# Output stores and x loads issued per half row of 128 tokens instead of per whole row

## The reference

```python
q = heads(x @ W_q)
probs_t = softmax(q @ heads(text @ W_k).T * scale)            # 73 text tokens
text_out = probs_t @ heads(text @ W_v)
attn_scores = q @ heads(ip @ W_k_ip).T * scale                # 4 ip tokens
sem = l2norm(probs_t @ text) @ l2norm(ip).T
probs_ip = softmax(attn_scores + 0.5 * sem) * spatial_mask
out = (text_out + probs_ip @ heads(ip @ W_v_ip)) @ W_out + b_out
out = out + x                                                 # the residual
```

## Time and profile before

| | before |
|---|---|
| time, median of 3 runs | 1032.5 us (1031.4 to 1037.69) |
| profiled execution, time | 1031.25 us |
| profiled execution, span | 1029.5 us |
| granted clock of the matrix engine, mean | 0.988 of full speed |
| matrix engine busy | 975.6 us (95%) |
| DVE, ACT, POOL busy | 795.9, 705.6, 640.5 us |
| queue q1 (all DMAs that SP issues) | 178.62 MB, 84.2% of 16 engines |
| output stores, x loads in the main loop | 64 and 56, 320 KB each |

### The profile page before, as it was taken

One profiled execution on the slowest core, in us unless ns is written; L12 is line 12 of the kernel. 1 busy time (PEld: TensorE's weight loads), 2 busy tenths in 40 slices (PEclk: granted clock), 3 DMA queues, 4 the chain that ended last, 5 costly groups with the idle time before them and its releaser, 6 DMA issues.

```text
span 1029.5 us, 24562 instructions
## 1 busy us (share of the span) xinstructions
PE 975.6 (95%) x7604; PEld 795.8 (77%) x7604; DVE 795.9 (77%) x2401; ACT 705.6 (69%) x2315; POOL 640.5 (62%) x1899
## 2 busy tenths in 40 slices
PE   7986788999999999999999999999999999999877
PEld 5755566888878888888878888888878888888755
DVE  4375678888878787888878888878888888887861
ACT  1355678777677777768767777777777777787720
POOL 1112467777676667667666767766766677676750
PEclk9999989999999999999999999999999999999989
DMA  9845989879799998888899999888989979778852
GB/s 301 316 139 138 193 152 169 172 167 186 159 190 177 188 190 174 164 176 172 158 189 194 189 167 184 160 177 168 178 179 202 180 169 186 138 160 147 159 109 89
DMA packets 483871, 180.26 MB, mean 175 GB/s; under 512 B 449517, under 2 KB 461855, under 8 KB 483740
## 3 DMA queue, kind: packets, MB, share of 16 engines
q1 hardware_dynamic: 483708, 178.62, 84.2%
q10 hardware_dynamic: 32, 0.07, 0.0%
HBM read 42.34 MB, written 27.22 MB: 68 GB/s over the span
## 4 chain that ended last, share of the span: by engine, by line
PE 77%; DMA 4%; DVE 3%; SPq 3%; ACT 2%; issue 2%; POOL 1%; POOLq 0%; DVEq 0%; ACTq 0%
PE ps_O L1164 26%; PE ps_Q L1198 25%; PE ps_S L1122 12%; PE ps_U L1184 11%; DMA pts<-ph 3%; PE ps_M L1138 3%; ACT pr L905 1%; SPq L825 1%; SPq L795 1%; DMA x_in<-in_x_dram 1%; SPq L785 0%; DVE pr L1060 0%; DVE n L1072 0%; POOL ph L987 0%; DVE w_sem L1055 0%
## 5 line engine op out<-in xcount | busy, mean ns | idle before, releaser
L987 POOL TENSOR_TENSOR ph<-pr,ph 128x220 f16<-128x220 f32 (+1 forms) x640 | 273.8, 459 | 136.5 <-ACT ph L917 136.2
L905 ACT ACTIVATE pr<-ps_S,bias 128x73 f32<-128x73 f32 x1280 | 290.1, 339 | 89.0 <-DVE bias L1021 87.0
L1164 PE MATMUL ps_O<-wo_hi,aT 128*128 128x320 f16 x1280 | 295.1, 302 | 5.6 <-DVE x_in L1006 3.5
L1198 PE MATMUL ps_Q<-xT,wq_hi 128*128 128x512 f32 x800 | 280.6, 416 | 5.9 <-DVE qT L994 5.7
L917 ACT ACTIVATE ph<-pr 128x292 f16<-128x292 f32 x640 | 234.2, 440 | 5.5 <-DMA pts<-ph 0.4
L1164 PE MATMUL ps_O<-wo_lo,aT 128*128 128x320 f16 x640 | 192.7, 301 | 0.0
L1184 PE MATMUL ps_U<-xm,pts 128*128 128x110 f16 (+1 forms) x2560 | 159.5, 213 | 17.9 <-DMA pts<-ph 15.4
L1198 PEld LDWEIGHTS ps_Q<-xT,wq_hi 128*128 128x128 f32 x800 | 146.5, 191 | 33.6 <-DVE qT L994 7.0
L1184 PEld LDWEIGHTS ps_U<-xm,pts 128*128 128x128 f16 (+1 forms) x2560 | 145.1, 98 | 34.9 <-issue 12.4
L1164 PEld LDWEIGHTS ps_O<-wo_hi,aT 128*128 128x128 f16 x1280 | 125.7, 98 | 57.4 <-DVE x_in L1006 4.0
L1122 PEld LDWEIGHTS ps_S<-kbd,qT 128*128 128x128 f32 x960 | 149.9, 189 | 23.2 <-issue 9.2
(11 more groups left out here) (185 smaller groups left out, 1235.3 us busy)
## 6 DMA issues: line engine op xcount, KB each, us to landing
out_dram<-x_in SPq DMA_DIRECT2D x64, 320.0 KB, 2.6
x_in<-in_x_dram SPq DMA_DIRECT2D x56, 320.0 KB, 3.2
pts<-ph SPq DMA_TRANSPOSE x320, 3.3
aT<-in_L_xattn_W_k_dram SPq DMA_DIRECT2D x5, 512.0 KB, 8.7
w_ip<-in_L_xattn_W_k_ip_dram SPq DMA_DIRECT2D x1, 2560.0 KB, 11.6
w_v<-in_L_xattn_W_v_dram SPq DMA_DIRECT2D x1, 2560.0 KB, 18.9
w_ip<-in_L_xattn_W_v_ip_dram SPq DMA_DIRECT2D x1, 2560.0 KB, 9.3
x_in<-in_x_dram SPq DMA_DIRECT2D x2, 1280.0 KB, 12.2
```

Source lines behind the costliest of these rows:

```text
L905: last = nc.scalar.activation(pr[p % P_RING][:, j, h, :], sc[:, j, h, 0:T], ACT.Exp, bias=bias[p % 2][:, j, h:h + 1], scale=SCALE)
L987: nc.gpsimd.tensor_tensor(lo, full[:, :, t0:t1], one[:, :, 0, t0:t1], ALU.subtract).then_inc(pl_ready, 1)
L1164: last = nc.tensor.matmul(o_bank[half % 2][:, 0:HALF], stationary, moving, start=(k, a, b_) == O_MMS[0], stop=(k, a, b_) == O_MMS[-1])
L1198: last = nc.tensor.matmul(ps_Q[:], wq[a][:, c, k * P:(k + 1) * P], xT[(CC * i + c) % XT_RING][b_][:], start=(c, a, b_) == Q_MMS[0], stop=( ...
```

## The change

Stores and loads are issued by halves: 128 partitions with 1280 bytes each, 160 KB, eight of each per tile. `STORE_AT` now has a step for each of the eight halves, one step behind the step in which DVE adds it, and `LOAD_AT` a step for each half of x, one step behind the store that frees its place. The last store and the last load of a tile stay in the steps in which the last rows were. Within a step the loads now come ahead of the stores, since a step often has both. The thresholds of the semaphores follow the new counts (`OUTS` for `SUB`). No computing instruction changes.

```diff
-    STORE_AT = {10: 0, 13: 1, 15: 2, 17: 3}
-    LOAD_AT = (-19, -16, -14, -12)
+    STORE_AT = {9: 0, 10: 1, 11: 2, 13: 3, 14: 4, 15: 5, 16: 6, 17: 7}
+    LOAD_AT = (-20, -19, -18, -16, -15, -14, -13, -12)
...
+    def half_of(tile, half):
+        return tile[:, half // 2, (half % 2) * HALF:(half % 2 + 1) * HALF]
...
+                for j in range(2, TILES):
+                    for half in range(OUTS):
+                        if p == max(STEPS * j + LOAD_AT[half], FIRST):
+                            if j >= X_RING:
+                                sp.wait_ge(x_stored[j % X_RING], 16 * (OUTS * (j // X_RING - 1) + half + 1))
+                            sp.dma_start(half_of(x_in[j % X_RING], half), half_of(rows(x, j), half)
+                                         ).then_inc(x_loaded[j % X_RING], 16)
                 for i in range(TILES):
                     if p - STEPS * (i + 1) in STORE_AT:
-                        q = STORE_AT[p - STEPS * (i + 1)]
-                        sp.wait_ge(o_added, OUTS * i + 2 * q + 2)
-                        sp.dma_start(rows(out, i)[:, q], x_in[i % X_RING][:, q, :]).then_inc(x_stored[i % X_RING], 16)
-                for j in range(2, TILES):
-                    for q in range(SUB):
-                        if p == max(STEPS * j + LOAD_AT[q], FIRST):
-                            if j >= X_RING:
-                                sp.wait_ge(x_stored[j % X_RING], 16 * (SUB * (j // X_RING - 1) + q + 1))
-                            sp.dma_start(x_in[j % X_RING][:, q], rows(x, j)[:, q]).then_inc(x_loaded[j % X_RING], 16)
+                        half = STORE_AT[p - STEPS * (i + 1)]
+                        sp.wait_ge(o_added, OUTS * i + half + 1)
+                        sp.dma_start(half_of(rows(out, i), half), half_of(x_in[i % X_RING], half)
+                                     ).then_inc(x_stored[i % X_RING], 16)
```

More of the change, by code:

```diff
@@ L855, in _ @@
             for r in range(X_RING):
-                sp.wait_ge(x_stored[r], 16 * SUB * B)
+                sp.wait_ge(x_stored[r], 16 * OUTS * B)
         @block.scalar
@@ L1131, in _ @@
                     if c == 0:
-                        pe.wait_ge(x_loaded[j % X_RING], 16 * (SUB * (j // X_RING + 1) if j % X_RING > 1 else SUB * (j // X_RING) + 1))
+                        pe.wait_ge(x_loaded[j % X_RING], 16 * (OUTS * (j // X_RING + 1) if j % X_RING > 1 else OUTS * (j // X_RING) + 1))
                     if j:
```

## The result

The changed kernel takes 1038.15 us (median of 20 runs, 1033.15 to 1044.14), the kernel before 1034.33 us in the runs beside it (20 runs, 1027.84 to 1037.69). The ratio is 1.0047 with a 95% interval of 1.0032 to 1.0063: slower by 4.9 us, with 3.3 to 6.5 us as bounds. This ratio isn't the quotient of the two medians, which is 1.0037 or 3.8 us; in the later runs, too, the two differ by up to 0.2%, most where a kernel ran only four or five times. The profiled execution took 1038.31 us, its span is 1036.5 us, 7 us longer than the span before; part of that is chance, as the experiments show.

The account below looks back on a forecast made before the run. PE sets the time, with SP's issue time the bound at the three batch borders: 6.2 (borders) + 0.4 (new wait) + 0.5 (start) - 0.3 (end) = 6.8 us on 1031.25, plus half the median's excess, gave 1038.6 us, range 1034 to 1042.8.

Parts of the forecast that it names:

- three signs that I had named for being wrong: Borders as short as before, PE's clock dropping in them, or the start shorter or longer by more than 2 us.
- What bounds it: PE sets the time; SP's issue time is covered inside a batch and is the bound at the three borders.
- The border term: Three borders between batches: added SP issues at 0.40 us each delay transposes; 1.8 + 2.6 + 1.8 = 6.2 us.
- PE's clock: Much slower rival: one clock fall at each border, 3 x 1.7 = 5.1 us on top, 1043.7 us; chance 0.19.
- The bound of zero: Borders: added issues only take time in which full DMA engines hold SP back, costing nothing; hidden rival, chance 0.20.
- The wait of a load for its half's store: Borders, steps 35, 37 and 41: SP may wait 0 to 0.5 us; 0.15 a border net, 0.4 us in all.
- The cover inside a batch: Inside a batch the added issues meet 1.2 to 2.5 us of SP slack per step and cost nothing.
- SP's waits for POOL: Inside batches SP waits for POOL to write `ph`; total lower by up to 48 us as added issues eat slack.
- The waits for `pts<-ph`: PE's waits for transposes: about 2 us more idle at each border, total about 22 us and not 15.4.
- The start: Added loads ahead of the transposes by step 4, more at steps 10 and 11; taken as 0.5 us lost.
- rival "faster": Halves let pieces ahead of the transposes come sooner; 1015.5 us if all such PE waits went; gain over 1%, chance 0.04.
- The end: The last store is 160 KB and lands sooner; gain 0 to 0.7 us, taken as 0.3.

Follow-up runs that it names:

- rows_at_border: The changed kernel with whole rows again for the tiles at the borders between batches, halves elsewhere; 1031.62 us, ratio to before 0.9976.
- halves_at_border: The kernel before with halves only for the tiles at the borders between batches, whole rows elsewhere; ratio to before 1.0054.
- two_rows: Against the kernel before: as many DMAs, but each takes half the columns of two rows, so all packets are 1280 bytes; ratio 1.0013.
- first_halves: The kernel before with whole rows, only the loads of tiles 2 and 3 at the start by halves; ratio to before 0.9986.
- first_late: The kernel before with whole rows, only the loads of tiles 2 and 3 at the start one step later; ratio to before 0.9977.
- twins: As many halves as the changed kernel, but both halves of a row in the same step, where the whole row was; ratio to before 1.0028.
- tiny_added: The kernel before plus one 2 KB DMA in each step where the changed kernel has one store or load more, 120 in all; ratio 1.0074.
- quarters: The changed kernel with stores and loads by quarters of a row (80 KB), two for each half; ratio to before 1.0479.
- before_again: The kernel before, unchanged, run for a second profile; ratio to before 0.9993.
- halves_kbd_act: The changed kernel with the 60 key loads (`kbd`) of the borders issued by ACT in place of SP; 1024.36 us, ratio to before 0.9916.

## Why the prediction was right, and where it wasn't

**The time.** 1038.6 us was forecast, 1038.15 is the median; the sum of the terms was +6.8 us, measured are +4.9 (3.3 to 6.5). The forecast time was met more closely than the difference, since the median of before is 1034.33 us over 20 runs and not the 1032.5 of the first three. The sum is 2 us too high, and that it is no more is partly luck: the start was off by 3.5 us one way and the borders by 1.4 the other. Of the three signs that I had named for being wrong, two came true: PE's clock dropped in the borders, and the start got shorter by more than 2 us.

**What bounds it** was right. SP is the bound at the borders and not inside a batch: rows_at_border takes the loss away, halves_at_border has it alone, and with the keys on ACT's queue PE has no idle time there.

**The border term**, 6.2 us for six added issues a border at 0.40 us each, less a margin at two borders, was right in cause and a little too small. The mean of the borders is 188.7 us over the six kernels with 320 KB pieces and `kbd` on SP's queue (before twice, rows_at_border, two_rows, first_halves, first_late), and 196.3 over the changed kernel, halves_at_border, twins and tiny_added: 7.6 us. Border by border the difference is 2.9, 2.8 and 1.8 us, where I had 1.8, 2.6 and 1.8. The wait of 1.97 us that made the second border special was chance: in the second profile of before, the waits there are 0.41 and 0.73 us. PE's idle time at the borders grew by 1.3 us each in the changed kernel, not the 2 that I had given as a sign. On SP, the time from the end of step 33's transposes to the end of step 41's, added up over the three borders, is 141.4 to 145.8 us in those six kernels and 152.9 to 155.2 in the four, 10.6 us more for 21 added issues, or 0.50 us each.

**PE's clock**, which I had set at nothing in the sum and named as a rival of its own, did fall, behind the waits at two of three borders: at the second one the wait grew from 1.97 to 2.70 us. The table books 4.3 us of clock in the four kernels and 0.9 in the six, 3.4 of the 7.6 us. But that is an account and not a cause. In the four kernels, the three borders without a fall took 64.5 to 65.4 us and the nine with one or two 64.8 to 66.4, only 0.6 us more in the mean, where the clock is booked with 1.9. Without any fall, the three took 64.9 in the mean and fifteen of the six kernels' 62.5: 2.4 us a border, or 7.2 of the 7.6 us. So the rival's price, 1.7 us a fall on top, and its 1043.7 us did not come. My reading is that SP sets the pace of a border and catches up while PE runs at the lower clock; no run tests that.

**The bound of zero** for this term, that the issues slip into time in which the DMA engines hold SP back, is refuted by tiny_added, by SP's 10.6 us, and by the share of 1.04 beside a fully busy PE. In the Trainium skill, "DMA: Bandwidth & Descriptors", section "Issuing engines are not separate DMA queues", the issue time is called usually small relative to the DMA itself. It is small here too; what failed at the borders is my step from small to nothing.

**The wait of a load for its half's store**, 0.4 us, is not there: SP's waits in the changed kernel have no row at L806. **The cover inside a batch** held: 181.65 of 182 us, 183.00 of 183, 178.96 of 179. SP's waits for POOL were to fall by up to 48 us and fell by 51, of which 9 went to waits under other names. **The waits for `pts<-ph`** were to rise to about 22 us and rose to 19.1.

**The start** is the step that failed: +0.5 us forecast, about -3 measured. I had written that the bytes issued by steps 1 and 4 are the same as before. That is true of the sum, and the sum is the wrong quantity: the transposes of step 4 have 160 KB ahead of them in their own step, where they had 320, and the other half went to step 2, where PE's two waits grew only from 1.17 to 1.85 us together, while those at pair 4 fell from 3.1 to 0.8. The rival "faster" named just this and was turned down by that sentence.

**The end**: 0.3 us gain forecast. Four kernels with whole rows in the last tile take 40.40 to 40.41 us, three with halves 40.02 to 40.03: 0.38 us. In twins, where both halves of the last row go out in one step, it is 40.50, and in quarters, with two issues for the last half, 40.32; so what gains is that only half a row is left to send at the very end. Before has 38.73, before_again 38.72 and halves_at_border 38.71. These three lack the stretch at the lower clock that begins 19 us behind pair 159 in each of the other ten kernels, and the ends differ by its price, 1.7 us; the 1.3 us by which the end looks longer after is that, less the gain. That before_again would have 38.7 us with two such stretches was half right: it has one, twice as long. By the fit in the Trainium skill, "DMA: Bandwidth & Descriptors", section on the anatomy of one DMA, half the bytes give 163840 / 436000 = 0.38 us, an estimate made there for DMAs issued from GpSimd, as are the 2.0 us of fixed cost that the prediction took from the same section; the runs agree with the 0.38.

The sum as it came out: 7.6 - 3.0 - 0.4 = 4.2 us by the profiles, 4.9 with 3.3 to 6.5 by the times.

## What to carry to other kernels

Halving a DMA doubles its issues, and what that costs is read from the queue that issues them: nothing where the issuing engine waits anyway, here 0.4 to 0.5 us an issue where it has no gap. Before cutting transfers smaller, look for the stretch in which the issuer is full, and either leave that stretch alone or move something else off the queue; the latter was worth nearly twice the whole question here. A byte sum over a stretch doesn't tell a wait: ask what stands ahead of the one transfer that is waited for, in its own step.

## What the runs showed of the hardware

A plain DMA on 128 partitions costs its issuer 0.36 to 0.44 us behind another one whether it moves 2 KB or 320 KB. At the borders SP is now and then held 0.7 to 1.4 us longer than usual at one issue, of whatever kind (a transpose of 2.7 us before, a store of 1.26 us after, a load of 1.11 us in tiny_added); what holds it is not shown. A DMA share of 1.01 to 1.04 over 65 us went with no wait of PE at all, so a share near 1 doesn't mean that the engines set the pace. PE's clock fell for 3.4 us at a time (now and then 6.8) behind waits of PE, but the size of the wait alone doesn't tell when: it fell behind 2.70 us in the changed kernel and behind 0.74 and 1.00 us in rows_at_border, and stayed up behind 1.97 us in before and 2.11 us in two_rows. Where SP set the pace, such a fall made a border longer by less than its 1.7 us. DMAs issued from ACT left its `ph` instructions at the median of before, 437 ns (halves_kbd_act).
